# Perceiver decoder kernel: a new order of the prologue's units and of the transfers that build the first key stack

## What is computed

```
scores = einsum('bhqd,bhkd->bhqk', q Wq, ctx Wk) / sqrt(16)
out    = einsum('bhqk,bhkd->bhqd', softmax(scores), ctx Wv) Wo
```

## Time and profile before

| what | us |
|---|---|
| median of 3 runs | 981.24 |
| the profiled execution | 982.42 |
| its span, first to last instruction | 980.6 |
| TensorE busy in the span | 905.7 |
| VectorE busy | 637.8 |
| ScalarE busy | 522.3 |
| GpSimd busy | 142.2 |

### The profile page before, as it was taken

The page is one execution under the profiler, slowest core; times in us unless marked ns, Lnnn a source line. Parts: engine busy times, 40 slices in busy tenths (PEclk is TensorE's granted clock), DMA queues, the critical chain, the costliest instruction groups (busy, mean ns, idle before and its releaser), DMA issues.

```text
span 980.6 us, 34386 instructions
## 1 busy us (share of the span) xinstructions
PE 905.7 (92%) x14880; PEld 577.1 (59%) x14880; DVE 637.8 (65%) x1105; ACT 522.3 (53%) x986; POOL 142.2 (15%) x175
## 2 busy tenths in 40 slices
PE   5578889899998999999999999999798999998998
PEld 2255556556665666666566566666443444447887
DVE  6547655667577556658666776777559677776622
ACT  5367756677676666666666746655652432103300
POOL 4212111111212121121211312211000000000000
PEclk9799999999999999999999999999999999999999
DMA  8676484635454534365254443425133233221200
GB/s 307 205 234 187 150 273 105 179 98 170 122 153 141 144 94 126 82 153 138 65 140 118 131 123 93 134 68 172 55 122 105 75 129 114 102 86 47 85 1 22
DMA packets 70839, 123.76 MB, mean 126 GB/s; under 512 B 34770, under 2 KB 46082, under 8 KB 67428
## 3 DMA queue, kind: packets, MB, share of 16 engines
q1 hardware_dynamic: 69812, 119.84, 41.2%
q0 software_dynamic: 592, 1.42, 0.4%
q10 hardware_dynamic: 288, 0.33, 0.1%
HBM read 64.88 MB, written 17.32 MB: 84 GB/s over the span
## 4 chain that ended last, share of the span: by engine, by line
PE 72%; DVE 12%; ACT 6%; issue 5%; SPq 3%; DMA 2%; POOL 0%; ACTq 0%; DVEq 0%
PE ps L748 71%; DVE mpart L1350 3%; SPq L523 3%; ACT p L1108 3%; DVE cl L1329 1%; DMA c32b<-in_ctxT 1%; ACT ch L1075 1%; DVE acc L1398 1%; ACT k L1091 1%; ACT kh L1092 1%; DVE v L1341 1%; PE ps L894 1%; DMA ks<-kh 1%; DVE w16a L1381 1%; DVE x L1450 0%
## 5 line engine op out<-in xcount | busy, mean ns | idle before, releaser
L1350 DVE TENSOR_REDUCE mpart<-ps 128x2 f32<-128x800 f32 (+1 forms) x256 | 252.5, 989 | 136.1 <-PE ps L748 134.3
L1108 ACT ACTIVATE p<-ps 128x512 f32<-128x512 f32 (+1 forms) x416 | 226.0, 597 | 180.4 <-PE ps L748 176.8
L703 POOL TENSOR_TENSOR kl<-k,kh 128x400 f16<-128x400 f32 (+1 forms) x128 | 119.4, 934 | 389.5 <-ACT kh L1092 389.5
L748 PE MATMUL ps<-p,v 128*17 128x64 f32 x6656 | 130.9, 221 | 0.0
L748 PEld LDWEIGHTS ps<-p,v 128*17 128x17 f32 x6656 | 97.6, 98 | 37.1 <-issue 36.3
L748 PE MATMUL ps<-wvh,ch 128*128 128x256 f16 (+1 forms) x416 | 115.2, 277 | 1.9 <-issue 1.9
L748 PE MATMUL ps<-wvl,ch 128*128 128x256 f16 (+1 forms) x416 | 114.1, 274 | 1.0 <-issue 1.0
L748 PE MATMUL ps<-wvh,cl 128*128 128x256 f16 (+1 forms) x416 | 114.1, 274 | 0.0
L748 PEld LDWEIGHTS ps<-qcur,ks 64*128 64x128 f16 (+1 forms) x3328 | 61.6, 97 | 71.7 <-issue 56.2
L748 PE MATMUL ps<-ch,wkh 128*128 128x400 f16 (+1 forms) x256 | 87.2, 341 | 14.2 <-ACT kh L1092 11.8
L748 PE MATMUL ps<-w16a,xmh 128*128 128x512 f16 x320 | 95.9, 381 | 3.5 <-DVE w16a L1381 3.5
(11 more groups left out here) (210 smaller groups left out, 1329.3 us busy)
## 6 DMA issues: line engine op xcount, KB each, us to landing
ks<-kh SPq DMA_DIRECT2D x256, 100.1 KB
w<-in_wgu SPq DMA_DIRECT2D x16, 1024.0 KB, 4.8
ks<-kl SPq DMA_DIRECT2D x128, 100.1 KB
w<-in_wd SPq DMA_DIRECT2D x8, 1024.0 KB, 4.7
c32a<-in_ctxT SPq DMA_DIRECT2D x16, 400.5 KB, 4.7
cparts<-ch SPq DMA_DIRECT2D x8, 800.5 KB, 6.6
cparts<-cl SPq DMA_DIRECT2D x8, 800.5 KB, 9.0
c32a<-in_ctxT SPq DMA_DIRECT2D x12, 400.0 KB, 3.2
```

The lines of the kernel that those rows point to most:

```text
L703: nc.gpsimd.tensor_tensor(kl[:, mt, k0:k0 + w], k32[:, ku % 2, 0:w], kh[:, mt, k0:k0 + w], ALU.subtract).then_inc(sem("klo_done"), 1)
L748: return nc.tensor.matmul(o, lhsT, rhs, start=start, stop=stop, skip_group_check=shared)
L1108: nc.scalar.activation(p32[0:n, step % PRING, BANK * side:BANK * side + BANK], ps[0:n, side, :], ACT.Exp, scale=DH ** -0.5).then_inc(sem(" ...
L1350: nc.vector.reduce_max(mpart[:, j0:j0 + 3:2, quarter], o.rearrange("p (b c) -> p b c", b=2)[:, :, 0:w], AX.X).then_inc(sem("max_done"), 1)
```

## The change

Three edits. The prologue's list takes K0 to K7 each with one P unit between them, then V0 and V1 among further P units, then N0 to N3 with the last P units. ScalarE splits the pieces 4 to 7 after K4, K6, V0 and V1; the list for VectorE is left as it is, so that VectorE still makes all four low parts of batch 1. SP issues restack(0, 0) straight after the stores of the queries, ahead of the loads of the queries of round 0, and of restack(0, 1) only the pairs 0 and 1 (6 transfers). The other 6 are issued by ScalarE after V0 (and its piece of context), behind a wait for the low parts of K4 to K7. The ones of the second stack and the stores of batch 0 move behind the loads of round 1's queries.

```diff
-PROLOGUE_UNITS = ("Q K0 K1 P0 P1 K2 P2 P3 K3 P4 V0 P5 P6 K4 P7 K5 P8 P9 K6 P10 V1 P11 K7 P12 P13 N0 P14 N1 P15 T N2 "
-                  "N3").split()
-FIRST_CTX_HIGH = {"K1": 4, "K3": 5, "V0": 6, "K4": 7}
+PROLOGUE_UNITS = ("Q K0 K1 P0 K2 P1 K3 P2 K4 P3 K5 P4 K6 P5 K7 P6 V0 P7 P8 V1 P9 P10 N0 P11 N1 P12 P13 N2 P14 N3 "
+                  "P15 T").split()
+FIRST_CTX_HIGH = {"K4": 4, "K6": 5, "V0": 6, "V1": 7}
 FIRST_CTX_LOW = {"P4": 4, "P6": 5, "P8": 6, "P10": 7}
...
-            def restack(r, mt):
+            def restack(r, mt, js=range(4)):
...
-                for j in range(4):
+                for j in js:
...
             load_stage(1)
             load(ks[0][0:P:PARTS, :, :], d["ones"], "ones_in0")
             store_queries(0, 0)
+            restack(0, 0)
             load_queries(0)
+            load_high_queries(1)
+            restack(0, 1, range(2))
+            load_queries(1)
             load(ks[1][0:P:PARTS, :, :], d["ones"], "ones_in1")
-            store_parts(0)
-            restack(0, 0)
-            load_high_queries(1)
-            load_queries(1)
-            restack(0, 1)
             load_ctx(8)
             load_ctx(9)
+            store_parts(0)
             store_parts(1)
             load_stage(2)
...
                 if name in FIRST_CTX_HIGH:
                     split_ctx(FIRST_CTX_HIGH[name])
+                if name == "V0":
+                    act.wait_ge(sem("klo_done"), K_UNITS)
+                    for j in range(2, 4):
+                        for n, part in enumerate((kh, kl, kh)):
+                            act.dma_start(ks[0][n + 1:P:PARTS, 4 + j, :], part[32 * j:32 * j + 32, 1, :])\
+                               .then_inc(sem("stacked1"), 16)
```

## The result

The changed kernel takes 976.79 us (median of 10 runs, 972.62 to 980.53) against 981.42 (10 runs, 980.17 to 983.42). The medians differ by 4.6 us; the ratio of the two kernels' runs is 0.9944, 95% interval 0.9928 to 0.9961, which is 5.5 us. By either the change is faster, clear of the 2 us that count as a difference. The forecast of 973.4 was 3.4 too low, inside the range. The runs spread wider than before, 8 us instead of 3. The profiled execution took 976.30 (span 974.3) and was 6.1 faster than the profiled one of before.

What follows compares the result with a forecast made beforehand. TensorE, busy 92%, was taken as the bound, with the stack's transfers gating the main loop's start. S 8.8 us earlier less 1.0 for the clock gave 7.8 net: 974.6 profiled, 973.4 for the median, range 969.5 to 978.0.

Steps and rivals of the forecast that it cites:

- The mechanism: Start of main loop: the stack's transfers gate S at 52.85; without that gate, VectorE's maxima and bank clearing set it.
- TensorE's times: Prologue on TensorE: K and P unit together take 1.40 us, putting K7 at 24.05 and V0 at 25.45.
- The part on SP: SP's prologue issues: first half of the stack issued by 29.2, SP's six of the second by 35.6, landed about 37.5.
- ScalarE's issues: ScalarE after V0: six stack transfers at 0.64 each, 3.85 us, of which 1.75 falls on the path.
- a clearing forecast at 42.7: VectorE before the main loop: last maximum ends at 39.6, and 3.05 later the bank is cleared.
- The clock: TensorE after idling from 38.7 to 42.7: a fall to 1.2 GHz costs 1.0 us, bounds 0 and 2.0.
- The sum: Start of S: 44.05, 8.8 us earlier than 52.85, less 1.0 for the fall to 1.2 GHz, net 7.8.
- The stack didn't remain the gate: Rival, chance 0.06: two queues share engines, issues stretch to 1.1 us each, S at 46.6, saving 5.3, 976.
- ScalarE wasn't stuck: Rival, chance 0.02: ScalarE's six issues take over 11.6 us and the kernel is slower; at 2.3 each, 983.4.
- The backlog in the loop: Rival, chance 0.17: 5.3 MB issued from 37 to 42 stalls the first steps, costing 4; saving 3.8, 977.4.
- The second queue: Six stack transfers on ScalarE: with all on SP the stack lands at 41.4, before V2 ends; saved issue time worth nothing.
- The unit order: Prologue order: VectorE idles some 2 us while K units run, paid later; its maxima and low parts stay the same work.

Runs made afterwards that it cites:

- the filled run: Changed kernel with V2's matmuls done three times more before TensorE waits for the cleared bank; 969.9 us, ratio 0.9875.
- the 36 small matmuls: Changed kernel with 36 fp16 matmuls of 32 by 16 on a zeroed tile added at TensorE's start; 973.0 us, ratio 0.9899.
- all on SP: Changed kernel with all twelve transfers of the first stack's second half issued by SP, none by ScalarE; 972.8 us, ratio 0.9910.
- SP's order alone: Kernel before with SP's issues in the change's order, all on SP, unit order as before; 975.5 us, ratio 0.9920.
- ScalarE's issues behind V1: Changed kernel with TensorE's bank wait moved to the first product with the values and ScalarE's six issues after V1 and piece 7; 972.0 us, ratio 0.9883.
- the best one: Changed kernel with later bank wait, ScalarE's six issues after V1 and piece 7, batch 0's stores before round 1's query loads; 968.7 us, ratio 0.9853.
- 144 fp32 matmuls: Changed kernel with 72 small fp32 matmuls added at TensorE's start, each shown as two in the trace; 1004.7 us, ratio 1.0214.

## Why the prediction was right, and where its sizes were off

**The mechanism** was right: the stack's issues gated S, and in the changed kernel VectorE's last maximum and the clearing do. TensorE's times came within 0.05 up to V0. The part on SP came out as worked: first half issued from 21.60 to 30.2 (29.2 forecast), SP's half ended at 36.7 (35.6), nothing waits for it.

**ScalarE's issues** were mis-sized a little: 4.3 for 3.85 behind the piece of context, 5.3 from the first issue to the end of the last. Two of them together took 2.53, while SP issued too. This and a few tenths elsewhere give 43.43 for a clearing forecast at 42.7; 0.25 of them are between the last maximum and the clearing (3.30 for 3.05).

**The clock** is the step that was off most: 2.35 where I put 1.0 between 0 and 2.0, so even the upper bound was too low. I took one 2 us stretch at half clock as the price. The half clock covered V2 and most of the first step, as the filled run shows. Nor is it a fixed price. After an idle stretch of the same 4.4 us V2 always lost 1.24, but the first step lost 0.31 with the 36 small matmuls, 1.11 in the changed kernel and 1.41 with all on SP: 1.55 to 2.65 together.

**The sum** was 7.8 for the profiled execution. The clearing 0.7 late and the clock 1.35 more make it 5.75; V2 started 0.11 behind the clearing and took 0.06 more at full clock than I had put, so 5.55, which is what the trace has at the second S and, at 5.50, in round 1. The profiled executions differ by 6.1, with TensorE's later "issue" waits shorter by 1.2. By the medians it gave 4.6, since the profiled run is 0.5 below its median and that of before was 1.0 above its own. The gain is thus 2.3 us (by the ratio) to 3.2 us (by the medians) smaller than forecast.

**The rivals.** The stack didn't remain the gate, and ScalarE wasn't stuck. The backlog in the loop did no harm in the changed kernel: its odd wait is the old one, at the same matmul. But it stood close behind. With S 2.8 earlier, in the run with SP's order alone, ScalarE waited 4.9 us for `cparts`.

**The second queue.** I had costed it as worth nothing and as a price of 1.75 us: with all on SP S came 1.5 earlier. The Trainium skill (DMA: Bandwidth & Descriptors, Issuing engines are not separate DMA queues) says that several issuing engines save only the sequencer's time, which is usually small beside the transfer. The outcome in the changed kernel agrees. But the stack's issues are not small here: to issue a transfer of 100 KB takes SP 0.60, and with the bank's wait out of the way TensorE waited 2.48 for a stack from one queue. S started no later for it (41.51 to 41.57 with two); two queues brought S forward, to 40.6, only with ScalarE's issues behind V1.

**What I missed.** The unit order was costed at nothing, with VectorE's idle time paid later. Alone it costs 2.5 us, since it puts the maxima behind the stack; and SP's order alone brings at least as much as the whole. I also took the wait for the cleared bank as given, though V2 doesn't write that bank. Moving it was the cheapest 5 us of the case.

## What to carry to other kernels

When a gate is removed, look at what stands behind it in the order of the program, not only at what is late next: here a wait for one PSUM bank stood ahead of a unit that uses another, invisible while a longer wait covered it. A new idle stretch on TensorE has its price in the work that follows, so cost everything that may run at half clock. And try the parts of a change alone: one of the three parts of this change cost 2.5 us by itself, another alone brought as much as the whole, and one queue was better than two as long as another wait stood behind it. A single trace can mislead by a few us for reasons that have nothing to do with the edit, such as the odd wait, so look for the matmul at which a difference arises.

## What was not expected of the hardware

TensorE waited 0.6 to 2.6 us in the middle of a unit for nothing that the trace shows, at the same matmul in eight of ten kernels with as many matmuls in front of it, and not there when 36 had been added ahead of it. Adding the 36 took 4.5 us off the changed kernel and nothing measurable off the best one. And 144 fp32 matmuls with 16 columns each took 30.9 us, 0.21 apiece: their small width didn't make them cheap. The matmuls of the queries' projection, with 128 columns, right behind them started 0.21 apart too. Both ran at the slow pace: the eight of the projection took 2.05 there and 1.13 in the loop at a granted clock of 1.00. The granted clock of the first 40 us of that trace reads 1.00 nevertheless, so there the length of a known matmul tells the pace and the record doesn't.
